# Stage edges, first loads and a normalisation moved in a seven-stage transformer kernel

## The reference

```python
x = x + attn_a(layernorm(x))     # q, k, v = x @ W.T; rotary on q and k; softmax(q k / 4) v @ Wo.T
x = x + moe(layernorm(x))        # router to 8 of 64 experts, 128 rows each at most, silu(g) * u,
                                 # plus one shared expert for all rows
x = x + attn_b(layernorm(x))     # phi = elu + 1 of q and k; f = sigmoid(x @ Wf.T + bf); per step
                                 # S = f S + phi_k v, z = f z + phi_k; out = phi_q S / (phi_q z + 1e-6)
x = x + moe(layernorm(x))        # the same mixture, the same weights

def _layernorm(x, axis=-1, eps=1e-05):
    m = jnp.mean(x, axis=axis, keepdims=True)
    v = jnp.var(x, axis=axis, keepdims=True)
    return (x - m) / jnp.sqrt(v + eps)
```

## Time and profile before

| | us |
|---|---|
| median of 3 runs | 2654.32 (2651.83 to 2654.82) |
| profiled execution | 2650.67 |
| its span, first to last instruction | 2648.7 |
| mean granted clock of TensorE | 0.958 of full |
| busy: TensorE / VectorE / ScalarE / POOL | 2432.0 / 1757.7 / 1265.9 / 1124.5 |

### The profile page before, as it was taken

How to read it: one execution, slowest core, us unless ns; L and a number is a source line. 1 busy time by engine, 2 the same in 40 slices (tenths; PEclk the granted TensorE clock), 3 DMA queues, 4 the chain that set the end, 5 groups by cost and what they waited for, 6 DMA issues and landing times. The chain is left out here.

```text
span 2648.7 us, 47571 instructions
## 1 busy us (share of the span) xinstructions
PE 2432.0 (92%) x14630; PEld 1346.6 (51%) x14630; DVE 1757.7 (66%) x3849; ACT 1265.9 (48%) x2564; POOL 1124.5 (42%) x1350
## 2 busy tenths in 40 slices
PE   8996899999999999979898995899999969898997
PEld 4664133333333333356556773466666646555775
DVE  7996888888888888368632323588888749833331
ACT  3443476767766776634322331455555414422332
POOL 6888200010000000023226675577777723325776
PEclk9998699999999999979998997999999989998999
DMA  5555433323232332046757884011111026775885
GB/s 168 175 185 179 113 96 90 100 84 96 83 97 87 93 91 65 29 144 199 238 179 195 223 195 74 9 38 37 38 37 36 21 68 206 237 213 155 219 222 98
DMA packets 289376, 325.33 MB, mean 123 GB/s; under 512 B 28944, under 2 KB 270752, under 8 KB 289184
## 3 DMA queue, kind: packets, MB, share of 16 engines
q1 hardware_dynamic: 257536, 274.49, 34.2%
q0 software_dynamic: 27136, 46.16, 8.5%
q10 hardware_dynamic: 4512, 2.40, 0.4%
HBM read 217.23 MB, written 105.19 MB: 122 GB/s over the span
## 5 line engine op out<-in xcount | busy, mean ns | idle before, releaser
L720 ACT ACTIVATE a_probs<-a_ps_s 128x512 f32<-128x512 f32 x1024 | 536.9, 603 | 281.5 <-PE a_ps_s L597 270.0
L672 DVE TENSOR_REDUCE a_row_max<-a_ps_m 128x2 f32<-128x1024 f32 x512 | 607.2, 1219 | 86.7 <-PE a_ps_m L571 82.4
L597 PE MATMUL a_ps_s<-a_qs,a_ks 98*128 98x512 bf16 (+1 forms) x1024 | 318.6, 390 | 7.9 <-ACT a_probs L720 6.5
L612 PE MATMUL a_ps_o<-a_probs,a_va 128*32 128x512 f32 x2048 | 272.4, 604 | 0.8 <-ACT a_o_sb L729 0.8
L1570 POOL TENSOR_TENSOR b_spread<-b_decay,held_own_sb 128x512 f32<-128x512 f32 x256 | 268.9, 1082 | 8.2 <-DVE b_weight L1668 8.2
L571 PE MATMUL a_ps_m<-a_ks,a_qs 48*128 48x512 bf16 x1024 | 206.7, 401 | 17.2 <-DVE a_row_max L672 11.4
L546 POOL DMA_DIRECT2D x<-a_xo x32 | 23.5, 734 | 435.1 <-DVE a_xo L705 435.1
L571 PEld LDWEIGHTS a_ps_m<-a_ks,a_qs 48*128 48x128 bf16 x1024 | 49.4, 93 | 309.6 <-issue 189.6
L1668 DVE TENSOR_TENSOR b_weight<-b_ps_s,b_spread 128x512 f32<-128x512 f32 x256 | 163.7, 681 | 17.6 <-PE b_ps_s L1805 17.6
L597 PEld LDWEIGHTS a_ps_s<-a_qs,a_ks 98*128 98x128 bf16 (+1 forms) x1024 | 76.4, 97 | 165.5 <-ACT a_probs L720 74.6
L517 POOL CAST a_high<-a_row_max 128x32 bf16<-128x32 f32 x32 | 6.6, 207 | 317.5 <-DVE a_row_max L672 317.5
(11 more groups left out here) (362 smaller groups left out, 5364.3 us busy)
## 6 DMA issues: line engine op xcount, KB each, us to landing
parts<-a_parts SPq DMA_DIRECT2D x16, 1536.0 KB, 6.2
a_qs<-parts SPq DMA_DIRECT2D x384, 64.0 KB, 2.2
a_ks<-parts SPq DMA_DIRECT2D x384, 64.0 KB, 2.2
rows<-m_early SPq DMA_DIRECT2D x32, 640.0 KB, 3.2
m_early<-x SPq DMA_DIRECT2D x32, 512.0 KB, 4.0
m_own<-in_L_ffn_w_gate_dram SPq DMA_DIRECT2D x24, 384.0 KB, 4.4
m_own<-in_L_ffn_w_up_dram SPq DMA_DIRECT2D x24, 384.0 KB, 5.7
m_own<-in_L_ffn_w_down_dram SPq DMA_DIRECT2D x24, 384.0 KB, 6.5
```

Of the source, the lines that this page charges most:

```text
L597: nc.tensor.matmul(s_bank(name, step)[:], ks[u][0:K_ALL[e], h, t * P:(t + 1) * P], qs[u][0:K_ALL[e], h, :], start=True, stop=True).then_in ...
L612: last = nc.tensor.matmul(ps_o[VW * j:VW * (j + 1), :], va[n.u][:, t, (h0 + j) * VW:(h0 + j + 1) * VW], probs[:, group % 2, j, t, :], star ...
L672: nc.vector.tensor_reduce(row_max[:, n.k // 4 % 2, t, :, n.p % 4], m_bank(name, step)[:], AX.X, ALU.max).then_inc(m_drained, 1)
L720: nc.scalar.activation(probs[:, group % 2, j, t, :], s_bank(name, step)[:], ACT.Exp, scale=DK ** -0.5).then_inc(s_drained, 1)
```

## The change

- **Block ends.** All seven blocks are opened with `no_gpsimd_drain=True`. Around the whole program stands one more `cleanup_on_exit`.
- **Stores waited for later.** Stage 1's stores of `parts` are waited for in stage 2 (by SP ahead of the sequences, by POOL ahead of its second set of memsets), stage 2's stores of x1 in the first mixture (by SP ahead of its last load, by ACT ahead of the first copy of the shared expert), and the shared expert's stores of both mixtures ahead of the first scatter. The waits for v, for the scatters and for forget attention's stores stay where they were.
- **First operands early.** SP loads the three first slots of sequence 0 in stage 1, 12 DMAs at tile 5 and 12 at tile 7, into `first_qs` and `first_ks`, which are stage 2's first buffers. Stage 1's `parts` and stage 2's second operand buffers share the tensor `second`.
- **Normalisation of stage 1.** ACT does it, as `Identity` with scale 1/σ and bias `shift`; `shift` = −mean/σ comes from a 128x1 tensor_scalar of DVE, `centre`.
- **Forget attention's operands.** The weights are turned at the end of the first mixture's experts, by PE into `ps_x` and `ps_t`, by ACT back over the loaded weights; DVE makes the masks there, at the end of its list. The setup of forget attention is gone. Its `v_aug` is cleared tile by tile on POOL at lag 1, for the first 12 tiles.
- **Ramp.** The first 8 tiles of forget attention are turned by `turn_early`, first in PE's step at lag 1, into `ps_w`, which is free then, and copied by ACT's `evacuate_early`; the later tiles as before.

The core of the diff:

```diff
-            walk(sp, TILES, TRIP, TRIP, [(0, load), (11, store_v), (14, store_parts)])
+            def load_first(n, k):
+
+                if isinstance(n, int) and n in (5, 7):
+                    sp.wait_ge(parts_stored[0], 16)
+                    for to, source in first_operands(dram["parts"], const["first_qs"], const["first_ks"], 0, n // 2 - 2):
+                        sp.dma_start(to, source).then_inc(first_in, 16)
+
+
+            walk(sp, TILES, TRIP, TRIP, [(0, load), (11, store_v), (14, store_parts), (14, load_first)])
+            sp.wait_ge(first_in, 16 * 24)
             for s in range(2):
                 sp.wait_ge(v_stored[s], 16 * SEQS // 2)
-                sp.wait_ge(parts_stored[s], 16 * SEQS // 2)
...
-            def normalise(n, k):
+            def centre(n, k):
                 j, u = k % TPB, k % 2
                 dve.wait_ge(rstd_done, n + 1)
-                wait(dve, x_turned, n - 3)
-                nc.vector.tensor_scalar(xn[:, j, :], xt[:, k, :], mean_var[:, j, 0:1], rstd[:, j],
-                                        ALU.subtract, ALU.mult).then_inc(xn_done, 1)
+                wait(dve, xn_done, n - 3)
+                nc.vector.tensor_scalar(shift[:, j], mean_var[:, j, 0:1], rstd[:, j], -1.0, ALU.mult, ALU.mult).then_inc(shift_done, 1)
...
-            walk(dve, TILES, TRIP, TRIP, [(0, statistics), (4, rotate), (6, remainder), (1, normalise)])
+            walk(dve, TILES, TRIP, TRIP, [(0, statistics), (4, rotate), (6, remainder), (1, centre)])
...
+            def normalise(n, k):
+                j, u = k % TPB, k % 2
+                act.wait_ge(shift_done, n + 1)
+                wait(act, x_turned, n - 3)
+                nc.scalar.activation(xn[:, j, :], xt[:, k, :], ACT.Identity, bias=shift[:, j], scale=rstd[:, j]).then_inc(xn_done, 1)
...
-            walk(act, TILES, TRIP, TRIP, [(7, middle), (2, evacuate_x), (3, evacuate_v), (5, high)])
+            walk(act, TILES, TRIP, TRIP, [(1, normalise), (7, middle), (2, evacuate_x), (3, evacuate_v), (5, high)])
...
-            for f in range(2):
-                load_qk(0, 0, f, range(MAX_SLOTS), first_loaded)
             sp.wait_ge(rows_set[0], 3)
             for f in range(2):
                 load_qk(0, 0, f, range(MAX_SLOTS, len(Q_PARTS)), rest_loaded)
+
+            for u in range(2):
+                sp.wait_ge(const["parts_stored"][u], 16 * SEQS // 2)
...
             walk_pairs(pool, [(L_TURN, split), (L_S, spread), (L_OUT[0] + 1, store(0)), (L_OUT[1] + 1, store(1))])
-            for q in range(2):
-                pool.wait_ge(stored[q], 16 * SEQS)
...
             sp.wait_ge(w_loaded, 48 * (OWN + EARLY_BUFFERS + KEPT_BUFFERS))
-            for k in range(2):
-                sp.wait_ge(stored[k], 16 * ROUNDS // 2)
...
             def scatter_first(i):
                 pool.wait_ge(y0_done, i + 1)
+                if i == 0:
+                    for k in range(2):
+                        pool.wait_ge(const[tag + "_shared_stored"][k], 16 * T // 1024)
...
+            def turn_b_weights(i):
+                if i < 2:
+                    pe.wait_ge((xT_done, hT_done)[i], PAIRS)
+                wait(pe, w_copied, i - 1)
+                bank = (ps_x, ps_t)[i % 2]
...
             def project_values(n):
                 sg, at = n // SG, n % SG * P
-                pe.wait_ge(xnT_done, min(n + L_VF - L_TURN, GROUPS))
+                pe.wait_ge(xnT_done, n + 1)
+                wait(pe, f_copied, n)
...
+            def turn_early(n):
+                if n < RAMP:
+                    pe.wait_ge(xn_done, n + 1)
+                    wait(pe, xnT_done, n)
+                    for c in range(2):
+                        last = nc.tensor.transpose(ps_w[:, c, :], xn[:, n % 4, c * P:(c + 1) * P], ident[:])
+                    last.then_inc(x_turned, 1)
...
-            in_turn([(L_VF, project_values), (L_S, scores), (L_PV, mix_values), (L_TURN, turn_x), (L_OUT, turn_output), (L_FEED, first_features),
+            in_turn([(L_TURN - 1, turn_early), (L_VF, project_values), (L_S, scores), (L_PV, mix_values), (L_TURN, turn_x), (L_OUT, turn_output), (L_FEED, first_features),
```

283 lines of the change are left out of this document (158 added, 125 removed).

## The result

The changed kernel takes 2630.96 us, the median of four runs (2628.56 to 2637.05). The kernel before takes 2653.07 on the same chip (2651.58 to 2654.82, four runs). The ratio is 0.992, 95% interval 0.9901 to 0.9938. So it is faster, but by 22 us and not by the 41 forecast, and it lies 2 us above the range. The profiled span is 2629.8 us against 2648.7, at a mean granted TensorE clock of 0.960 against 0.958.

What follows compares the result with a forecast made beforehand. The prediction took VectorE to set stage 1's pace and nothing to work at the stage edges. Its terms summed to 41.2 us, so the median of 2654.3 became 2613, with a range from 2600 to 2629.

Steps and rivals of the forecast that it cites:

- Stage 1: Stage 1's pace: 3.46 to 3.31 us a tile with normalisation on ScalarE, less 1.0 at the start; 8.5 us gained.
- (b): Rival, stage 1: it gains nothing, as the normalisation adds two hand-overs to the loop; total 2621.5 us, chance 0.12.
- Edge 1 to 2: Stage 1 to stage 2: SP waits only for the values, stage 2 starts at 247.9 instead of 253.09; 5.2 us gained.
- The loads left out: Stage 2's start: SP issues 48 small loads instead of 72, but first waits for three memsets; 0.6 us gained.
- Front to experts: Both mixtures: VectorE no longer idles for SP's last store, awaited before the first scatter; 2.3 us each, 4.7 together.
- Experts to forget attention and its setup: Forget attention's start: 4.6 us gained without the GpSimd drain, 10.2 as first statistics wait only for x.
- The ramp: Forget attention's first tiles: early turns bring first features 2.4 us earlier, the next two steps lose 4.0; net −1.
- The end: Program's end: 5.0 us less without the drain, about 1.0 more for another clearing of semaphores; 4.0 gained.
- (a): Rival, edges behind POOL's DMAs: the drain is not what costs 4 us; 11.2 less gained, 2624 us, chance 0.11.
- (d): Rival, stage 1: VectorE's centre waits for POOL's rotation sum in every tile, 4.5 us a tile; 2688 us, chance 0.05.
- (c): Rival: stage 1 at 3.27 us a tile and the ramp keeps its lead; total 2606.5 us, chance 0.08.
- (e): Rival, whole kernel: removed waits come back as others, nearly all gain lost; within 5 us of before, chance 0.02.

Runs made afterwards that it cites:

- e2: The kernel before with 92 more waits (46 instructions) at the end of ScalarE's stage 1, stage 2 body from the 320th: 2678.04 us, ratio 1.007.
- e1: The changed kernel with 32 more waits (16 instructions) at the end of ScalarE's stage 1, stage 2 body from the 336th: 2605.74 us, ratio 0.9815.
- e4: The changed kernel with stage 1's normalisation back on VectorE and no centre operation, ScalarE's stage 2 body from the 275th: 2622.14 us, ratio 0.9876.
- e8: e6 with SP loading sequence 0's maxima rows ahead of the next sequence's operands, waits moved to stage 2's start: 2599.96 us, ratio 0.98.
- e5: e1 with the GpSimd drain back at the end of all blocks: 2614.07 us, ratio 0.9847.
- e9: e1 with no tile of forget attention turned early (RAMP 0 instead of 8): 2612.44 us, ratio 0.9804.
- e6: e1 with six instead of eight tiles of forget attention turned early: 2597.77 us, ratio 0.9789.
- e7: The changed kernel with 512 more waits (256 instructions) at the start of ScalarE's stage 2, body from the 576th: 2628.5 us, ratio 0.9902.
- e3: The kernel before with 124 more waits (62 instructions) at the end of ScalarE's stage 1, stage 2 body from the 336th: 2646.46 us, ratio 0.9972.

## Why the prediction was wrong

**The step that failed** is the one that has no term: the sum takes stage 2 from its first scores to its last store at its old 838 us, and gives no reason for it. It became 862. What failed is the reading of the change as a set of edits that act where they stand; ScalarE's 46 more instructions in stage 1 act in stage 2, by shifting its loop body to just ahead of a border between pieces of code. e2 makes this from the kernel before alone, e1 takes it away from the changed one. With e1 the whole gain is 48.6 us in the medians and 43.9 in the spans, where 41.2 was summed. The closeness is in part luck: 2.6 of the 43.9 come from stage 2's middle, where e1 also loses the old stall, and the mixtures gain 4.7 and lose 2.0 where the sum has 2.3 gained in each. The trace of before did hold hints that the prediction passed over: ScalarE's stall of about 2 us behind each jump, and instructions fetched five times in every turn of a loop.

**Stage 1 (8.5).** The last store of `parts` is issued at 237.13 instead of 246.03, 8.9 earlier, and e4 against e1 gives 7.9. The pace is 3.30 (3.31 taken). ScalarE's normalisation takes 0.60 us, not 0.4, which nothing waits for but the first tile's turn: the first copy comes at 17.4 instead of 16.30, 1.1 lost where 1.0 was taken. Rival (b), no gain, is out.

**Edge 1 to 2 (5.2).** From the store's issue to POOL's first instruction 1.85 us instead of 7.06: 5.2. **The loads left out (0.6):** 0.4. SP was to take the removed loads' place and did; `load_m` is issued at 272.26, and e8 shows that SP's queue held the scores by 1.9 us.

**Edge to the mixture (4.4):** 5.0; the drain alone is 3.3 of it by e5. **Front to experts (4.7 for two):** at the edge of mixture 1 VectorE's idle time goes from 3.53 to 1.31, 2.2 (2.3 taken), and at that of mixture 2 from 3.25 to 1.30, 2.0.

**Experts to forget attention and its setup (4.6 and 10.2).** Together 14.5. The rows of the changed kernel, from the last scatter to the first features and TensorE's next turns, against the earlier trace rows:

```profile
1618.60 1.94 POOL L1327 DMA_INDIRECT x<-m1e_y,m1e_slots  x1 [0.30 <-issue]
1624.03 0.10 POOL L1640 MEMSET b_minus_half<- 128x1 f32 x1 [3.49 <-POOLq L1995]
1626.67 0.43 DVE L1680 BATCH_NORM_STATS2 b_stats<-b_xt 128x6 f32<-128x256 f32 x1 [5.91 <-DMA b_xt<-x]
...
1628.82 0.69 PE L1832 MATMUL b_ps_w<-held_ident_sb,b_xn 128*128 128x128 f32 x2 [10.24 <-DVE b_xn L1690]
...
1638.87 1.08 PE L1824 MATMUL b_ps_a<-held_b_w_v,b_xnT 128*128 128x272 f32 x4
1639.79 1.02 PE L1856 MATMUL b_ps_p<-b_xnT,held_b_w_q 128*128 128x512 f32 x2
...
1645.58 0.49 PE L1832 MATMUL b_ps_w<-held_ident_sb,b_xn 128*128 128x128 f32 x2 [3.91 <-DVE b_xn L1690]
...
1647.90 1.69 PE L1856 MATMUL b_ps_p<-b_xnT,held_b_w_q 128*128 128x512 f32 x2
...
1654.37 0.69 PE L1832 MATMUL b_ps_w<-held_ident_sb,b_xn 128*128 128x128 f32 x2 [3.91 <-DVE b_xn L1690]
```

The stage starts 5.4 us behind the scatter, where it was 9.8 (1634.27 − 1624.51): 4.3. The first statistics come 2.64 behind the start instead of 12.8: 10.2. The transposes and masks did stay hidden; TensorE has been idle for 10.24 us at its first turn.

**The ramp (a loss of 1, from 2.4 won and 4.0 lost): the net was right by luck, as both parts were too small.** The loss came out as 1.2 (39.62 to 40.85). The sum's own two parts make a loss of 1.6, and the prediction doesn't say why it takes 1. The first features come 11.0 us after the first turn, not 13.9: the sum took each projection at the slow rate of before, but TensorE is at full clock from 1636 on (0.55 in the 4 us before), while the kernel before still had 0.50 there from 1656 to 1664, so the last projections take 1.08 instead of the 2.02 of the first. With the waits of e1 in both, the first features come 13.4 us behind the first statistics with eight early turns (1605.03 to 1618.46) and 18.4 with none (e9): 5.0 earlier, where 2.4 was summed. What was given back is the mechanism named: the turns at 1645.58 and 1654.37 wait 3.91 us for normalisations that stand behind the features in VectorE's step. It was priced at 4.0 for two steps. From e9's and e1's rows it is 7.1, as 5.0 were won by the first features and 2.1 lost by the fifth; from the given kernels' it is 6.6, of 5.4 won and 1.2 lost. With these waits TensorE is busy for 1.6 to 2.5 us in each 4 from 1640 to 1656, and its granted clock falls to half twice, from 1645.8 to 1649.2 and from 1652.7 to 1659.5. The features take 1.69 and, at 1656.89, 1.91 instead of 1.10. The stretches around the second fall:

```profile
1652.00:1656.00 4.00, 1.64 (x6) 1.34 (x7) 2.25 (x5) 0.93 (x2) 0.98 (x4) 0.58 0.00 0
1656.00:1660.00 4.00, 4.00 (x9) 2.22 (x7) 0.00 (x0) 0.79 (x3) 0.63 (x2) 0.56 0.00 0
```

**The end (4.0):** 4.3; with the drain it is 5.0 longer (e5). The 1.0 that the sum takes for one more clearing of semaphores is shown by no run by itself; e5, which has the drain and the added clearing, is 0.4 longer there than the kernel before (10.2 for 9.7).

**The rivals.** (a) is out by e5, (b) by e4, (d) by the centre's 0.20 us. (c) was an idea of more gain by a faster stage 1 and a ramp that keeps its lead; neither came by itself, the second came with e6. (e), the removed waits coming back as others, fell too: nothing removed came back. What took half of the gain was on no list, since all of them asked what becomes late at the place of an edit.

## What to carry to other kernels

When an edit adds instructions to an engine ahead of a loop, compare where the loop's body begins in that engine's whole instruction list, look in the profile for an engine that stands for some 2 us behind each jump, whatever releaser is named, and for packets of the kind "instruction" in a steady loop; some waiting instructions that do nothing can be worth more than the edit (here 16 of them gave 25 us). A stall of 1.4 to 1.7 us on an engine that TensorE waits for cost 1.8 us here where TensorE's granted clock held, and up to 4.8 where it fell behind the stall. Early work in a ramp should end where the next step's first instruction would depend on something that stands late in another engine's step: six turns gained 4.4 us where eight gained nothing.

## What the runs showed of the hardware

- A jump back to a loop body of 313 instructions on ScalarE costs nothing that shows when the body begins at the 336th instruction, 1 us when at the 274th or 304th, 1.4 to 4.4 at the 314th and 2.5 to 6.5 at the 320th (steps of 37.57, 38.5, 39.0 to 42.0 and 40.1 to 44.0 us), and the same 256 instructions further on (e7).
- Behind it are fetches of code: 5 packets of 8192 bytes in each steady turn where it costs (before, after, e2, e7), none where it doesn't (e1, e3, e6). In the kernel before, those away from the jump lie 43 us apart.
- TensorE's granted clock fell to half (1.2 GHz) for 6.8 us behind a stretch in which TensorE was busy for 1.91 of 4 us (after, 548 to 552); behind the first jump, with the same two stalls and 1.75 of 4 us busy (442 to 446), it did not fall.
- The GpSimd drain at a block's end costs 3.3 to 5.0 us behind stages whose last DMAs POOL issued, and nothing that can be seen behind those whose last DMAs are SP's (e5).
- A tensor_scalar of 128x1 beside POOL's tensor_tensor takes 0.20 us and isn't blocked, while the 128x256 one took 0.98 instead of 0.42. ScalarE's activation with a scale and a bias for each partition takes 0.60 us for 128x256 from SBUF, its plain copy of as much from PSUM 0.36 to 0.38.
